# Last stage of an audio-tower kernel: halves made before the transposition, DMA transposes of four blocks, and a second layer in three f16 products

## What is computed

```python
h = tok(x)                              # window attention over tokens, projection: (128, 127, 192)
h = h + attn(layernorm(h))              # 8 heads, three concatenated halves, projection
h = h + ffn(layernorm(h))

def ffn(x):                             # the stage that is changed
    logits = x @ router_w + router_b    # 4 experts
    idx = argmax(softmax(logits))
    dispatch = one_hot(idx, 4)
    h = gelu(einsum('bsd,edh->besh', x, w1) + b1)      # 192 -> 4 x 192
    y = einsum('besh,ehd->besd', h, w2) + b2
    return einsum('besd,bse->bsd', y, dispatch) + x
```

## Time and profile before

| | us |
|---|---|
| median of 3 runs | 2323.7 (2322.72 to 2324.74) |
| profiled execution, its time | 2322.24 |
| its span, first to last instruction | 2320.5 |
| the last stage, from its first instruction (1605.3) | 715.2 |
| busy: TensorE, VectorE, ScalarE, GpSimd | 2162.2, 1419.9, 1354.7, 974.6 |
| mean granted TensorE clock, of 1.0 = 2.4 GHz | 0.974 |

### The profile page before, as it was taken

How to read it: one execution, slowest core, us unless ns; L and a number is a source line. 1 busy time by engine, 2 the same in 40 slices (tenths; PEclk the granted TensorE clock), 3 DMA queues, 4 the chain that set the end, 5 groups by cost and what they waited for, 6 DMA issues and landing times. The chain is left out here.

```text
span 2320.5 us, 60046 instructions
## 1 busy us (share of the span) xinstructions
PE 2162.2 (93%) x20736; PEld 1303.8 (56%) x20736; DVE 1419.9 (61%) x3727; ACT 1354.7 (58%) x3042; POOL 974.6 (42%) x1815
## 2 busy tenths in 40 slices
PE   5999999849999999999999999993999999999996
PEld 4999999714444444444444444441656655665563
DVE  4555555449999999999999999981222222222221
ACT  1333333328888888888888888882343344334331
POOL 1111111267777777777777777754111011101100
PEclk9999999959999999999999999996999999999998
DMA  5444344124444444444444444440000000000000
GB/s 147 122 110 133 109 122 122 55 39 88 86 89 87 86 87 88 86 87 87 87 87 87 87 87 87 87 74 4 15 19 18 18 19 18 18 19 18 18 18 20
DMA packets 443152, 158.63 MB, mean 68 GB/s; under 512 B 383456, under 2 KB 442475, under 8 KB 443115
## 3 DMA queue, kind: packets, MB, share of 16 engines
q1 hardware_dynamic: 443115, 158.15, 30.9%
HBM read 53.31 MB, written 12.48 MB: 28 GB/s over the span
## 5 line engine op out<-in xcount | busy, mean ns | idle before, releaser
L699 DVE TENSOR_REDUCE tops<-p_maxa 128x6 f32<-128x762 f32 x512 | 482.9, 943 | 83.1 <-PE p_maxa L542 83.0
L538 PE MATMUL p_s<-qm,kt 32*128 32x256 f16 x3072 | 433.3, 276 | 1.3 <-ACT probs L656 0.6
L613 PE MATMUL p_o<-probs,vn 127*32 127x256 f32 x6144 | 412.1, 386 | 0.2 <-DVE att L727 0.2
L654 ACT ACTIVATE probs<-p_s 128x512 f32<-128x512 f32 x512 | 305.7, 597 | 144.4 <-PE p_s L538 114.0
L940 ACT ACTIVATE gel<-f_w,b 128x512 f32<-128x512 f32 x192 | 131.9, 687 | 416.2 <-PE f_w L892 414.1
L701 DVE TENSOR_REDUCE tops<-p_maxb 128x4 f32<-128x508 f32 x512 | 345.8, 675 | 0.0
L1016 POOL TENSOR_TENSOR f_res<-h,f_hn 128x192 f32<-128x192 f32 x128 | 75.5, 590 | 584.1 <-DVE out_sb L989 426.9
L542 PE MATMUL p_maxa<-kt,qt 24*128 24x256 f16 (+1 forms) x2048 | 293.7, 250 | 24.0 <-issue 19.2
L538 PEld LDWEIGHTS p_s<-qm,kt 32*128 32x128 f16 x3072 | 163.3, 91 | 269.2 <-issue 112.7
L659 ACT ACTIVATE probs<-p_s 128x512 f32<-128x512 f32 x512 | 309.9, 605 | 0.0
L656 ACT ACTIVATE probs<-p_s 128x512 f32<-128x512 f32 x512 | 303.3, 592 | 0.0
(11 more groups left out here) (185 smaller groups left out, 4397.0 us busy)
## 6 DMA issues: line engine op xcount, KB each, us to landing
xn<-in_xn SPq DMA_DIRECT2D x32, 768.0 KB, 6.3
xt_a<-in_xt SPq DMA_DIRECT2D x32, 512.0 KB, 4.3
out<-out_sb SPq DMA_DIRECT2D x32, 381.0 KB
xt_b<-in_xt SPq DMA_DIRECT2D x32, 256.0 KB, 5.2
xt<-hx SPq DMA_TRANSPOSE x128, 2.4
kt<-qk SPq DMA_TRANSPOSE x128, 2.8
qt<-qk SPq DMA_TRANSPOSE x128, 2.4
qm<-qk SPq DMA_TRANSPOSE x128, 2.8
```

The lines of the kernel that those rows point to most:

```text
L538: return nc.tensor.matmul(o, kt[full(j), r, kind, g, :], qm[full(j), r % 2, versions, g, :], start=True, stop=True, skip_group_check=True)
L613: last = nc.tensor.matmul(p_o[32 * j:32 * j + 32, blocks, :], vn[0:NP, r, src:src + 32], probs[0:NP, r % 2, QUAD * g + j, kind * 256:(kind ...
L654: nc.scalar.activation(probs[:, r % 2, h:h + 2, 512:768], p_s5[:, :, :].rearrange("p (h x) n -> p h (x n)", h=2), ACT.Exp, scale=SCALE).th ...
L699: nc.vector.tensor_reduce(top[:, q, pair, 4:10], p_ma[:, 0:6, 0:NP], AX.X, ALU.max, negate=True).then_inc(dve_ma[u], 1)
```

## The change

`setup` loads third parts of the router's and the first layer's weights and a 128-row `b2`, makes f16 halves of `w2`, and GpSimd writes the `far` rows (now 2^15, f16) into the free lower half of the first layer's fourth weight tile. In `feed_forward`, now prepared two groups ahead in rings of U = 4:

- GpSimd makes from `hn` (one normalization of 192 columns now) the high and the low half side by side (`hx`, 384 columns of f16 a block), the residual, and the 64 last columns of the high half in `pk`, beside which VectorE's `choose` writes mask and one-hot columns.
- SyncE issues a DMA transpose of `hx` for all four blocks (12 pieces, `xt`) and one of `pk` (4 pieces, `pkt`). TensorE's transposes and the copies behind them are gone.
- The first layer has five matmuls a chunk (the last on `pkt`, which holds the mask rows too).
- ScalarE does gelu in f32 (two buffers) and copies it to f16 (`ghi`), VectorE makes the low half (`glo`); the second layer runs chunk by chunk, two chunks behind the first layer, as three f16 products a block and chunk, with one bias matmul a block.
- The store keeps its shape; it stands in SyncE's body before the two transposes.

```diff
 def setup(nc, t, dram):
+        w2f = sb("w2f", [128, HCH, C], F32)
+        b2f = sb("b2f", [128, C], F32)
...
+            nc.vector.tensor_copy(t.w2_hi[:, :, :], w2f[:, :, :])
+            nc.vector.tensor_copy(t.b2[:, :], b2f[:, :])
...
+            nc.vector.tensor_tensor(t.w2_lo[:, :, :], w2f[:, :, :], t.w2_hi[:, :, :], ALU.subtract)
...
 def feed_forward(nc, t, dram, NB):
...
+        @block.sync
+        def _(sp):
...
+            def body(i, r, half):
+                if within(i - 1, NG):
+                    ready(dve_y, seen(i * G))
+                    dst = dram["out"][bass.ds(i - 1, 1), :, :, :].rearrange("g b p d -> p (g b) d")
+                    sp.dma_start(dst, out_sb[0:NP, (r - 1) % 2, :, :]).then_inc(stored[(r - 1) % 2], 16)
+                if within(i + 1, NG):
+                    ready(dve_pick, seen(i + 2))
+                    ready(pool_x, seen((i + 2) * G))
+                    if within(i - 1, NG):
+                        ready(pe_w[HCH - 1], seen(i))
+                        ready(pe_w2[0], seen(i))
+                    sp.dma_start_transpose(pkt[:, (r + 1) % 2], pk[:, (r + 1) % U].rearrange("p g n -> p (g n)")).then_inc(dma_pk, 16)
+                if within(i + 2, NG):
+                    ready(pool_x, seen((i + 3) * G))
+                    if within(i - 2, NG):
+                        ready(pe_w[HCH - 1], seen(i - 1))
+                    sp.dma_start_transpose(xt[:, (r + 2) % U].rearrange("p g k n -> p (g k) n"),
+                                           hx[:, r % 2].rearrange("p g n -> p (g n)")).then_inc(dma_x, 16)
...
+            def up(i, r, c):
+                if within(i, NG):
+                    if c == 0:
+                        pe.wait_ge(dma_x, seen(16 * (i + 1)))
+                        pe.wait_ge(dma_pk, seen(16 * (i + 1)))
+                    if c >= 3:
+                        pe.wait_ge(act_g[c - 3], seen(i + 1))
+                    else:
+                        pe.wait_ge(act_g[c + 3], seen(i))
+                    cols = slice(c * 128, (c + 1) * 128)
+                    x, o = xt[:, r], p_w[c % 3][:, :]
+                    nc.tensor.matmul(o, wa[:, cols], x[:, :, 0, :], start=True, stop=False)
...
+                    nc.tensor.matmul(o, wbl[:, cols], pkt[:, r % 2], start=False, stop=True).then_inc(pe_w[c], 1)
+
+            def down(g, ring, c):
+                if within(g, NG):
+                    pe.wait_ge(dve_lo[c], seen(g + 1))
+                    for k in range(G):
+                        o, n = p_y[k][:, 0:C], slice(k * 128, (k + 1) * 128)
+                        if c == 0:
+                            pe.wait_ge(dve_y, seen((g - 1) * G + k + 1))
+                            nc.tensor.matmul(o, pkt[:, ring, k, :], t.b2[:, :], start=True, stop=False)
+                        nc.tensor.matmul(o, ghi[:, c % 3, n], t.w2_hi[:, c, :], start=False, stop=False)
+                        nc.tensor.matmul(o, ghi[:, c % 3, n], t.w2_lo[:, c, :], start=False, stop=False)
+                        last = nc.tensor.matmul(o, glo[:, c % 3, n], t.w2_hi[:, c, :], start=False, stop=(c == HCH - 1))
...
+            def body(i, r, half):
                 for c in range(HCH):
+                    up(i, r, c)
+                    if c == 0:
+                        router(i, r)
+                    if c < 2:
+                        down(i - 1, (r - 1) % 2, c + HCH - 2)
+                    else:
+                        down(i, r % 2, c - 2)
...
         @block.scalar
+                        nc.scalar.activation(gel[:, c % 2, :], p_w[c % 3][:, :], ACT.Gelu, bias=t.b1[:, c:c + 1]).then_inc(act_g[c], 1)
+                        act.wait_ge(act_g[c], seen(i + 1))
...
+                        nc.scalar.activation(ghi[:, c % 3, :], gel[:, c % 2, :], ACT.Copy).then_inc(act_hi[c], 1)
...
         @block.vector
+            def body(i, r, half):
+                low(i, 0)
+                choose(i, r)
+                low(i, 1)
                 for k in range(G):
+                    output(i, r, half, k)
+                for c in range(2, HCH):
+                    low(i, c)
...
         @block.gpsimd
+                    nc.gpsimd.tensor_tensor(x[:, 0:C], hn[:, k % 2, :], one[:, :].broadcast_to([128, C]), ALU.mult).then_inc(pool_hi, 1)
+                    nc.gpsimd.tensor_tensor(res[:, ring, k, :], t.h[:, bass.ds(n * C, C)], hn[:, k % 2, :], ALU.add)
+                    nc.gpsimd.tensor_tensor(pk[:, ring, k, 0:CB], hn[:, k % 2, CA:C], one[:, :].broadcast_to([128, CB]), ALU.mult)
+                    pool.wait_ge(pool_hi, seen(n + 1))
+                    nc.gpsimd.tensor_tensor(x[:, C:2 * C], hn[:, k % 2, :], x[:, 0:C], ALU.subtract).then_inc(pool_x, 1)
```

More of the change, by code:

```diff
@@ L130, in _ @@
[L130 to L136 removed]
+            dve.wait_ge(high, 1)
@@ new lines, in _ @@
+            for name, (a, b, c) in splits:
+                rows = CB if name == "w1" else 128
+                nc.vector.tensor_tensor(t.split[name][1][:, :], a[:, :], t.split[name][0][:, :], ALU.subtract)
+                nc.vector.tensor_tensor(t.split[name][3][0:rows, :], b[0:rows, :], t.split[name][2][0:rows, :], ALU.subtract)
+            nc.vector.tensor_tensor(t.w2_lo[:, :, :], w2f[:, :, :], t.w2_hi[:, :, :], ALU.subtract)
+            nc.vector.tensor_tensor(t.b2[96:128, :], b2f[96:128, :], t.b2[96:128, :], ALU.subtract)
@@ L826, in loop @@
         def loop(eng, body):
[L828 to L835, removed]
+            for i in range(-2, 3):
+                body(i, i % U, (i - 1) // 2)
+            rounds = (NG - 5) // U
+            with eng.Fori(0, rounds) as j:
+                for r in range(U):
+                    body(j * U + (3 + r), (3 + r) % U, j * 2 + (2 + r) // 2)
@@ new lines, in loop, with ready @@
+            for i in range(3 + U * rounds, NG + 1):
+                body(i, i % U, (i - 1) // 2)
+        @block.sync
+        def _(sp):
+            def ready(signal, count):
+                sp.wait_ge(signal, count)
+                sp.sem_inc(sp_ready, 1)
+            def body(i, r, half):
[16 more added lines that the diff above has]
+                                           hx[:, r % 2].rearrange("p g n -> p (g n)")).then_inc(dma_x, 16)
+            loop(sp, body)
+            for par in range(2):
+                sp.wait_ge(stored[par], 16 * ((NG + 1 - par) // 2))
@@ L850, in router @@
[L850 to L870, removed]
@@ L872, in body @@
-            def body(i, par, half):
-                for c in range(HCH):
[L874 to L891, removed]
-                        nc.tensor.matmul(o, far[:, c * 128:(c + 1) * 128], pick_t[:, par].rearrange("p g n -> p (g n)"),
-                                         start=False, stop=True).then_inc(pe_w[c], 1)
-                    if c < G:
-                        rows_t(i, par, c)
-                router(i, par)
-                for k in range(G):
-                    if within(i, NG):
-                        n = i * G + k
-                        if k == 0:
-                            for c in range(HCH):
-                                pe.wait_ge(act_g[c], seen(i + 1))
-                        pe.wait_ge(dve_y, seen(n - 1))
-                        o = p_y[k % 2][:, 0:C]
-                        for c in range(HCH):
-                            nc.tensor.matmul(o, gel[:, c, k * 128:(k + 1) * 128], t.w2[:, c, :], start=(c == 0), stop=False)
-                        nc.tensor.matmul(o, pick_t[:, par, k, :], t.b2_hi[:, :], start=False, stop=False)
-                        nc.tensor.matmul(o, pick_t[:, par, k, :], t.b2_lo[:, :], start=False, stop=True).then_inc(pe_y, 1)
-                    if k == 2:
-                        picks_t(i, par)
@@ new lines, in _, with router @@
+            (wa, wal, wb, wbl), wc = t.split["w1"], t.third["w1"]
+            (ra, ral, rb, rbl), rc = t.split["wrouter"], t.third["wrouter"]
+            def router(i, r):
+                if within(i + 1, NG):
+                    pe.wait_ge(dma_x, seen(16 * (i + 2)))
+                    pe.wait_ge(steps[0], seen(i + 1))
+                    for k in range(G):
+                        x = xt[:, (r + 1) % U, k]
+                        o = p_log[:, k, :]
+                        nc.tensor.matmul(o, x[:, 0, :], ra[:, :], start=True, stop=False)
+                        nc.tensor.matmul(o, x[:, 0, :], ral[:, :], start=False, stop=False)
+                        nc.tensor.matmul(o, x[:, 1, :], rb[:, :], start=False, stop=False)
+                        nc.tensor.matmul(o, x[:, 1, :], rbl[:, :], start=False, stop=False)
+                        last = nc.tensor.matmul(o, x[:, 2, :], rc[:, :], start=False, stop=True)
+                    last.then_inc(pe_log, 1)
@@ new lines, in choose, with output @@
+                nc.vector.tensor_scalar(pk[:, (r + 1) % U, :, 64:68], pk[:, (r + 1) % U, :, 68:72], -1.0, FAR, ALU.add, ALU.mult)\
+                    .then_inc(dve_pick, 1)
+            def output(i, r, half, k):
+                if within(i - 1, NG):
```

(34 more changed lines are left out.)

226 lines of the change are left out of this document (92 added, 134 removed).

## The result

The changed kernel takes 2555.5 us (median of 4 runs, 2552.55 to 2560.83) against 2323.2 before: a ratio of 1.100, 95% interval 1.098 to 1.103, slower by 232 us. The prediction was 2568, in a range of 2480 to 2650. The profiled execution took 2557.35 us, its span is 2555.6.

The account below looks back on a forecast made before the run. The bound: a loop in which masks' transposes wait behind one-engine stores, period 29.3 us. Body 1 at 1640.5, 30 periods (879 us) to 2519.5, last stores to 2564.9, then the median: 2568 us, range 2480 to 2650.

Parts of the forecast that it names:

- The sum for TensorE: Last stage, per group: first layer 6.6 us, second 6.4, router 0.5, together 13.5 us at full clock against 21.34 before.
- The store on one engine: Last stage: a store of 127 partitions runs on a single DMA engine, 390,144 bytes at 23 GB/s, 17.0 us.
- The transposes wait for it, in the order of the queue: SyncE's queue: transposes behind a store wait until it is through; masks land 19.9 us after the store's issue.
- From the body's start to the store: Last stage: from body i's start, TensorE at half clock at first, to the issue of group i-1's store, 9.4 us.
- The period: Last stage: 9.4 us to the store's issue plus 19.9 to the next masks, 29.3 us a group against 21.34.
- the step from span to median: End of the sum: execution time 1.7 us above its span and 1.5 below the median, as before the change.
- The fill and the setup: Setup 4 us longer, stage starting at 1609.3; filling and body 0 take 31.2 us, so body 1 begins at 1640.5.
- The end: Kernel's end: group 30's store lands 19.0 us after issue, the last queues behind it for 17.0, ending at 2564.9.
- The halves' transpose at no cost: Last stage: the halves land 1.6 us after the masks, under the first chunk, adding nothing to the period.
- Rival 1: Last stage: the store does not hold up the transposes; the store alone binds, period 17.3 us, 2207 us; chance 0.11.
- Rival 2: Last stage: successive stores also use different engines and overlap; TensorE binds at 13.5 us a group, 2085 us; chance 0.05.

Follow-up runs that it names:

- the cut store: The changed kernel with its store issued as two DMAs of 112 and 15 partitions, nothing else changed: 2086.4 us, 0.899 of before.
- the best version: The changed kernel with its store split into 112 and 15 partitions and VectorE's outputs ahead of chunk 1's low half: 2072.8 us, 0.892 of before.
- the run with the masks first: The changed kernel with only the masks' transpose moved ahead of the store in SyncE's body, the halves' transpose staying behind it: 2532.4 us.
- the cut at 61 rows: The changed kernel with its store issued as two DMAs of 66 and then 61 partitions: 2312.2 us.
- the matmuls on constant data: The changed kernel with 54 unused matmuls of 512 columns on TensorE ahead of its wait for the transposes, from group 2 on: 2501.8 us.

## Why the prediction was right

- *The sum for TensorE.* 13.5 us a group without the store: 14.1 measured with the cut store, 13.7 in the best version. The matmuls were priced rightly: without their waits of 0.7 and 0.2 us for the outputs, ahead of the bias rows, which the sum took as hidden, 13.4 and 13.5 are left.
- *The store on one engine.* Share 0.07 and 23 GB/s again. Shown by the cuts.
- *The transposes wait for it, in the order of the queue.* This was the step with two far ends, 0 and 19 us, and the upper end was taken by the earlier trace rows. Masks landed 19.1 us after their own issue, 19.7 after the store's (0.55 between both issues); 19.9 was forecast. Shown by the size of the part on one engine, by the order in the queue, and by the other queue. The picture behind it, one part of the transpose that waits on the store's engine, is not what most of the time goes to: SyncE's issue takes 15.3 us instead of 1.2, and only the last 3.8 us lie behind it, where some 1.5 are usual (2.7 less 1.2, with the cut store). So of 16.4 us of delay 14.1 are a held issue and 2.3 come after it. The end of both follows the bytes on the one engine (issues of 15.3, 7.1 and 1.2 us for 127, 61 and no rows on it), so the number came out; how the store's engine holds an issue was not tried and stays open.
- *From the body's start to the store.* Forecast 9.4; measured 8.7 in one body (1989.10 to 1997.78) and 9.8 in the next (2017.55 to 2027.33), 9.2 in the mean. The difference is the clock: the prediction took 5 us at half clock from the earlier trace rows, which every second body has (5.2 us), and the others have only 3.4. There the 12 matmuls of chunk 4 of the second layer, 2.0 us at half clock by the sum, took 1.35 (1991.76 to 1993.11); in the next body 1.87 (2020.21 to 2022.08).
- *The period.* 29.04 for 29.3, 9.2 and 19.8 us (from the store's issue to the next body's first matmul, 1997.78 to 2017.55) for 9.4 and 19.9. Over the 30 periods, 1649.18 to 2519.39, that is 870 us for 879, 9 of the 12.5 us between forecast and result. Another 3 are the step from span to median: the profiled execution lay 1.9 us above the median, and the forecast took it 1.5 below, as before the change.
- *The fill and the setup.* First store forecast at 1649.9 (1640.5 + 9.4), measured 1649.18. The setup grew by 3.8 us (first load of the next stage at 25.94 instead of 22.16), 4 forecast.
- *The end.* From the issue of the second last store, 2519.39, to the end of the span 36.2 us; 36.0 forecast.
- *The halves' transpose at no cost.* Right in the changed kernel, but only as cover: it would have cost the same 13 us had the masks come early, as the run with the masks first shows. The prediction did not say so.
- *Rivals.* Rival 1, the transposes not held, falls with the landing of 19.1 us. Rival 2, stores on engines in turns, needs the same and falls with it, and with the cut at 61 rows, where it would have given some 2100 us.

The mechanism of the prediction stands in what it forecast: the masks land when the store ahead of them in the queue is through, and the loop closes over that. This was only argued then and is shown now; where the time is spent, mostly in the issue, it did not have. Of the page "DMA: Bandwidth & Descriptors" of the Trainium skill the prediction used two rules. That 127 partitions give one engine stands in the section "Why a DMA increments its semaphore by 16 and not by 1", not in the one that the prediction names; the trace agrees (share 0.07, 23 GB/s; with 112 partitions 336 KB land in 2.7 us, over 120 GB/s, where the one engine moved 23). That an engine consumes descriptors in ring order stands in the section "Queues, rings and completion order"; the landings agree with it, but no run here tells it apart from the held issue. The section "Issuing engines are not separate DMA queues" says that DMAs of different issuing engines interleave; the trace agrees, with a price: beside a store in ScalarE's queue the transposes take 5.5 and 9.3 us instead of 2.7 and 3.7.

## What to carry to other kernels

A transfer that nobody waits for is free only while nothing needed stands behind it in its queue. Before DMAs are put into a queue that holds a long one, read how many engines that one uses (share of the DMA time while it is alone, 0.07 here, about 1/16) and cut it so that it spreads over more: 112 + 15 partitions instead of 127 took 469 us off this kernel, and the order of issue alone 292. A long total in the waits names the engine at the end of a ring of waits; look for the one whose release comes from outside.

## What was not expected of the hardware

SyncE itself is held in the issue of the transpose behind a store: 15.3 us, where 1.2 is usual, and 7.1 behind 61 rows on one engine. With the store last, the issue is 7.1 us behind the store and takes 8.7; in both cases it ends 15.8 us after the store's issue (1790.54 to 1806.34, and 1795.21 to 1811.05). So nothing else could be issued from this queue either in that time. While the issue is held, the transpose moves nothing on the 15 engines that the store leaves free: the DMA share stays at 0.07 until 2013.

And successive periods of the changed kernel alternate: 29.57 us between the stores at 1765.64 and 1795.21, 28.54 to the next at 1823.75. It is the clock: half for 5.2 us in one body and 3.4 in the next, 1.8 us more at half speed, worth some 0.9. With the matmuls on constant data, which keep the clock at 1.00, the periods are 27.25 and 27.26. Why the clock rises sooner in every second body no run shows.
